# Two transformer layers in one kernel: the last part staggered by one pair, and the recurrence's running sums spread over more banks, without fillers

## The reference

```python
k_h = softmax(k_t W_in) * lr;  q_h = softmax(q_t W_in)
o_t = q_h W_out + (causal(q_h k_h^T)) v_t
W_out += k_h^T v_t
for _ in range(2):
    g_out, g_in = -attn(W_in, k_t, v_t), -attn(W_out, v_t, k_t)
    W_in, W_out = W_in - lr_in * g_in, W_out - lr_out * g_out
```

## Time and profile before

| | us |
|---|---|
| median of three runs | 2673.7 |
| the profiled execution | 2678.2 |
| its span | 2676.4 |
| TensorE busy | 2314.9 (86%) |
| VectorE busy | 1603.7 (60%) |
| ScalarE busy | 1575.9 (59%) |
| GpSimd busy | 1095.1 (41%) |
| fillers in the last part (line 966, 960 records) | 202.5 |
| fillers in the recurrence (line 814, 544 records) | 151.7 |

### The profile page before, as it was taken

One profiled execution on the slowest core, in us unless ns is written; L12 is line 12 of the kernel. 1 busy time (PEld: TensorE's weight loads), 2 busy tenths in 40 slices (PEclk: granted clock), 3 DMA queues, 4 the chain that ended last, 5 costly groups with the idle time before them and its releaser, 6 DMA issues.

```text
span 2676.4 us, 90848 instructions
## 1 busy us (share of the span) xinstructions
PE 2314.9 (86%) x33549; PEld 1456.5 (54%) x33549; DVE 1603.7 (60%) x3880; ACT 1575.9 (59%) x4079; POOL 1095.1 (41%) x1208
## 2 busy tenths in 40 slices
PE   5999994788887878886699999999999999999998
PEld 4545542455555555554367475564655656647566
DVE  2888885666666666665265474663744736537365
ACT  1878885666656666665264483563835737447365
POOL 0122221566666666667423344133332343323423
PEclk8999997888988998998899999999999999999999
DMA  5455556523322323311421302202132022220220
GB/s 173 138 156 159 156 170 143 101 51 80 78 65 67 77 64 79 74 29 33 126 48 49 88 23 78 48 26 88 30 94 47 26 70 48 76 66 26 70 48 17
DMA packets 404872, 206.35 MB, mean 77 GB/s; under 512 B 273938, under 2 KB 389778, under 8 KB 404388
## 3 DMA queue, kind: packets, MB, share of 16 engines
q1 hardware_dynamic: 404420, 200.37, 28.4%
HBM read 106.38 MB, written 71.38 MB: 66 GB/s over the span
## 4 chain that ended last, share of the span: by engine, by line
issue 33%; PE 33%; POOL 15%; DVE 9%; ACT 5%; DMA 2%; SPq 1%; POOLq 0%; DVEq 0%; ACTq 0%
POOL arena L1654 7%; PE psum L747 6%; PE psum L835 3%; DVE arena L1719 3%; PE psum L830 3%; PE psum L1013 3%; PE psum L1021 3%; ACT arena L1261 2%; PE psum L823 2%; PE psum L843 2%; PE psum L814 2%; POOL arena L1666 1%; PE psum L973 1%; PE psum L1004 1%; DVE arena L1728 1%
## 5 line engine op out<-in xcount | busy, mean ns | idle before, releaser
L1654 POOL TENSOR_TENSOR arena<-arena 128x400 f32<-128x400 f32 x256 | 218.2, 853 | 492.1 <-DVE arena L2029 492.1
L1261 ACT ACTIVATE arena<-psum,scan_sb 64x128 f32<-64x128 f32 x1152 | 308.1, 361 | 148.6 <-PE psum L904 82.7
L1445 ACT ACTIVATE arena<-psum,arena 128x100 f32<-128x100 f32 x1024 | 269.8, 366 | 6.6 <-DVE arena L2021 6.6
L1719 DVE SCALAR_TENSOR_TENSOR arena<-psum,taps_sb,arena 128x511 f32<-128x511 f32 (+2 forms) x288 | 213.7, 747 | 60.6 <-ACT arena L1170 53.8
L747 PE MATMUL psum<-arena,w_in_sb 128*128 128x512 f32 x512 | 229.9, 598 | 0.9 <-issue 0.9
L1477 POOL TENSOR_TENSOR arena<-arena 128x512 f32<-128x512 f32 x64 | 79.5, 1272 | 360.9 <-ACT arena L1196 360.9
L1501 POOL TENSOR_TENSOR arena<-arena 128x512 f32<-128x512 f32 x132 | 139.6, 1057 | 209.3 <-ACT arena L1289 209.2
L1786 DVE TENSOR_TENSOR arena<-psum,scan_sb 64x512 f32<-64x512 f32 x290 | 186.1, 674 | 36.0 <-PE psum L922 28.8
L966 PE MATMUL psum<-mask_sb,identb 128*128 128x400 bf16 x960 | 202.5, 347 | 0.0
L1437 ACT ACTIVATE arena<-psum 100x512 f32<-100x512 f32 x256 | 156.1, 610 | 49.3 <-PE psum L1087 43.0
L2021 DVE TENSOR_REDUCE arena<-psum 128x4 f32<-128x400 f32 x256 | 146.3, 573 | 62.5 <-PE psum L1074 50.8
(11 more groups left out here) (212 smaller groups left out, 4926.4 us busy)
## 6 DMA issues: line engine op xcount, KB each, us to landing
arena<-arena SPq DMA_DIRECT2D x144, 128.0 KB
arena<-x SPq DMA_DIRECT2D x32, 512.0 KB, 4.1
arena<-gates_d SPq DMA_DIRECT2D x116, 128.0 KB, 4.5
arena<-o_d SPq DMA_DIRECT2D x18, 512.0 KB, 7.3
arena<-gate_d SPq DMA_DIRECT2D x18, 512.0 KB, 8.4
v_rows_d<-arena SPq DMA_DIRECT2D x64, 136.0 KB
k_rows_d<-arena SPq DMA_DIRECT2D x64, 136.0 KB
arena<-k_rows_d SPq DMA_DIRECT2D x128, 68.0 KB, 2.0
```

The source lines that it names most:

```text
L1261: ins = act.activation(dst.rearrange("p (t x a) -> p t x a", x=PP, a=INNER)[upper, :, x], src.rearrange("p (t a) -> p t a", a=INNER)[upper ...
L1445: act.activation(c_soft[s][:, f % 2, u], sc, ACT.Exp, bias=c_max[s][:, u:u + 1]).then_inc(c_act.mark(f"exp{s}{f}u{u}"), 1)
L1654: pool.tensor_tensor(soft, soft, c_rec[s].unsqueeze(2).broadcast_to([P, 4, KEYS]), ALU.mult).then_inc(c_pool.mark(f"prob{s}{f}"), 1)
L1719: ins = dve.scalar_tensor_tensor(out=a_acc[:, t, j:TOK], in0=bank[2 + t][:, 0:TOK - j], scalar=taps_sb[:, t % KT, col:col + 1], in1=a_acc[ ...
```

## The change

In the last part the head of a pair (output projection, residual, statistics, normalisation, turn, modulation) is taken out into functions `next_...` that run for pair i + 1 inside pair i. TensorE does the projection of the next pair (`next_out`) between the down-projection and norm 2, VectorE its residual and statistics (`next_rows`) behind norm 2, and its normal form (`next_normal`) behind the mixing of layer 1; TensorE's turns (`next_turn`) stand before each slot's `vv`. The next pair has buffers of its own for its rows and statistics. SP loads the next rows after this pair's second residual, and outputs and weights during or after the attention. The first head runs before the loop, and the last pair is written out behind the loop without a successor. The turns of norm 2 go to banks 1 and 2 and stand before both value products. In a pair with a successor 58 of the 120 fillers go: those of norm 1, u1, norm 2 and vt. The fillers of the attention and of norm 3 stay. The copies that filled past sequences at the start are gone.

In the recurrence all fillers go. The sums use banks 6, 7, 5, 6, where bank 5 was the fillers'. `sums(2)` stands where sums 0 and 1 stood, `sums(3)` where 2 stood, and sums 1 and 0 of the next chunk stand in the waits at the end of a chunk; `add_state` for 2 and 3 is cut in two. GpSimd makes its products before its outputs, VectorE's mean of the outputs moves behind the maxima, and ScalarE evicts 3 before 2.

```diff
+        RUN_BANKS = (6, 7, 5, 6)
...
+            def pair(i, before, ahead, ahead2):
+
+                if before:
+                    store_rows(i - 1)
+                    load_gates_ffn(i)
+                    load_gates(i, "wv", c_wv, 3)
+                if ahead:
+                    for s in SLOTS:
+                        sp.wait_ge(c_dve.sem, c_dve.at(i, f"x2{s}1"))
+                        hold(sp)
+                        load_rows(i + 1, s)
+                    sp.wait_ge(n_pool.sem, n_pool.at(i + 1, "oz1"))
+                    hold(sp)
+                frame_values(i)
+                if ahead2:
+                    next_weights(i + 2)
+                if ahead:
...
+                            load_outputs(s, i * 2 + s + 2 * len(SLOTS))
+                    sp.wait_ge(c_pe.sem, c_pe.at(i, "wp11"))
+                    hold(sp)
+                    load_gates(i + 1, "wp", c_wp, 2)
...
-                    keep_busy(4)
...
-                    pe.wait_ge(act.sem, act.before(c, "rv3"))
-                    pe.wait_ge(pool.sem, pool.before(c, "kv0"))
-                    sums(0)
-                    pe.wait_ge(pool.sem, pool.before(c, "kv1"))
-                    sums(1)
+                    pe.wait_ge(act.sem, act.before(c, "rv2"))
+                    pe.wait_ge(pool.sem, pool.before(c, "kv2"))
+                    sums(2)
                     pe.wait_ge(act.sem, act.at(c, "e2"))
...
-                    keep_busy(1)
                     pe.wait_ge(dve.sem, dve.at(c, "wok"))
...
+
                     pe.wait_ge(act.sem, act.at(c, "rv0"))
-                    pe.wait_ge(pool.sem, pool.before(c, "kv2"))
-                    sums(2)
-                    keep_busy(1)
+                    pe.wait_ge(pool.sem, pool.before(c, "kv3"))
+                    sums(3).then_inc(mine.mark("sm3"), 1)
                     pe.wait_ge(dve.sem, dve.at(c, "xo"))
...
-                    pe.wait_ge(act.sem, act.at(c, "rv1"))
-                    pe.wait_ge(pool.sem, pool.before(c, "kv3"))
-                    sums(3)
-                    keep_busy(1)
                     pe.wait_ge(act.sem, act.at(c, "eb0"))
                     pe.transpose(bank[2][:, 3 * P:4 * P], e_b[:, 0], ident[:]).then_inc(mine.mark("tb0"), 1)
+                    add_state((2, 3), before_last, (0, 1))
                     pe.wait_ge(act.sem, act.at(c, "eb1"))
                     pe.transpose(bank[1][:, 3 * P:4 * P], e_b[:, 1], ident[:]).then_inc(mine.mark("tb1"), 1)
-                    add_state((2, 3), before_last).then_inc(mine.mark("r23"), 1)
-                    keep_busy(2)
-                    for r, b in enumerate((3, 0)):
-                        pe.wait_ge(dve.sem, dve.at(c, f"xb{r}"))
-                        pe.wait_ge(act.sem, act.at(c, f"xb{r}"))
-                        updates(grid(bank[b][:, 0:PP * ROW17], ROW17), pb_in[r], k_rows[i % 2], every).then_inc(mine.mark(f"pb{r}"), 1)
-                    keep_busy(3)
+                    pe.wait_ge(dve.sem, dve.at(c, "xb0"))
+                    pe.wait_ge(act.sem, act.at(c, "xb0"))
+                    updates(grid(bank[3][:, 0:PP * ROW17], ROW17), pb_in[0], k_rows[i % 2], every).then_inc(mine.mark("pb0"), 1)
+                    add_state((2, 3), before_last, (2, 3)).then_inc(mine.mark("r23"), 1)
+                    pe.wait_ge(dve.sem, dve.at(c, "xb1"))
+                    pe.wait_ge(act.sem, act.at(c, "xb1"))
+                    updates(grid(bank[0][:, 0:PP * ROW17], ROW17), pb_in[1], k_rows[i % 2], every).then_inc(mine.mark("pb1"), 1)
                     pe.wait_ge(dve.sem, dve.at(c, "wi1"))
                     pe.transpose(bank[2][:, 0:P], w_in_1, ident[:]).then_inc(mine.mark("ti1"), 1)
-                    keep_busy(3)
+                    pe.wait_ge(act.sem, act.at(c, "rv1"))
+                    pe.wait_ge(pool.sem, pool.at(c, "kv1"))
+                    sums(1)
                     pe.wait_ge(dve.sem, dve.at(c, "wi"))
                     pe.transpose(bank[1][:, 0:P], w_in_now, ident[:]).then_inc(mine.mark("ti"), 1)
-
-            pe.wait_ge(re_act.sem, re_act.at(CHUNKS - 1, "rv3"))
+                    pe.wait_ge(act.sem, act.at(c, "rv3"))
+                    pe.wait_ge(pool.sem, pool.at(c, "kv0"))
...
+            def next_out(n):
+
+                for s in SLOTS:
+                    pe.wait_ge(n_pool.sem, n_pool.at(n, f"wo{s}"))
+                    pe.wait_ge(n_pool.sem, n_pool.at(n, f"oz{s}"))
+                    rows_out(s, n_pe, "wo", lambda k, t: c_oz[s][:, k, tok(t)], lambda k: c_wo[s][:, k], (3, 0))
+
+            def next_turn(n, s):
+
+                pe.wait_ge(n_dve.sem, n_dve.at(n, f"xh{s}3"))
+                turn_rows(s, n_pe, "t", (2, 3))
...
+
+                for s in SLOTS:
+                    pe.wait_ge(n_act.sem, n_act.at(i, f"h{s}1"))
...
-                for s in SLOTS:
-                    pe.wait_ge(c_pool.sem, c_pool.before(i, f"wo{s}"))
-                    pe.wait_ge(c_pool.sem, c_pool.before(i, f"oz{s}"))
-                    pe.wait_ge(c_act.sem, c_act.before(i, f"kk{s}1"))
-                    rows_out(s, "wo", lambda k, t: c_oz[s][:, k, tok(t)], lambda k: c_wo[s][:, k], (2, 3))
...
-                for s in SLOTS:
-                    if s == 0:
-                        pe.wait_ge(c_dve.sem, c_dve.before(i, "rv11"))
-                        stay_warm("norm1", B(1, 1))
-                    turn_c(s, 1, (0, 1))
-                    stay_warm(f"u1{s}", B(1, 0) if s == 0 else B(0, 1))
-                    pe.wait_ge(c_act.sem, c_act.at(i, f"h1{s}1"))
-                    for k in range(KT):
-                        mm = pe.matmul(B(s, 0)[half(s)], u1_sb[:, k], c_h[s][:, k, 1:TOK + 1], start=(k == 0), stop=(k == KT - 1))
+                        mm = pe.matmul(B(s, 3)[half(s)], u1_sb[:, k], c_h[s][:, k, 1:TOK + 1], start=(k == 0), stop=(k == KT - 1))
                     mm.then_inc(c_pe.mark(f"u1{s}"), 1)
+                for s in SLOTS:
+                    pe.wait_ge(c_dve.sem, c_dve.before(i, f"rv{s}1"))
...
                                 mm.then_inc(c_pe.mark(f"v2{s}{a}"), 1)
-                for s in SLOTS:
-                    if s == 0:
-                        stay_warm("norm2", B(1, 0))
-                    turn_c(s, 2, (3, 0))
-                    stay_warm(f"vt{s}", B(1, 0) if s == 0 else B(0, 3))
+                if ahead:
+                    next_out(i + 1)
+                else:
+                    stay_warm("norm2", B(1, 0))
+                for s in SLOTS:
+                    turn_c(s, 2, (1, 2))
+                for s in SLOTS:
...
                 for s in SLOTS:
+                    if ahead:
+                        pe.wait_ge(c_act.sem, c_act.at(i, f"kk{s}1"))
+                        next_turn(i + 1, s)
                     pe.wait_ge(c_pool.sem, c_pool.at(i, f"kk{s}1"))
                     pe.wait_ge(c_act.sem, c_act.at(i, f"r{s}1"))
                     pe.wait_ge(c_pool.sem, c_pool.at(i, f"wv{s}"))
-                    rows_out(s, "vv", lambda k, t: c_kk[s][:, k, tok(t)], lambda k: c_wv[s][:, k], (0, 1))
+                    rows_out(s, c_pe, "vv", lambda k, t: c_kk[s][:, k, tok(t)], lambda k: c_wv[s][:, k], (0, 1))
+
+            with pe.Fori(0, LAST) as i:
+                pair(i, True)
...
+                        pool.wait_ge(pe.sem, pe.at(c, "sm3" if j == 3 else "r01"))
                         if j == 0:
...
+                    products(0)
+                    products(1)
                     outputs(0)
                     outputs(1)
-                    products(0)
-                    products(1)
...
+                    products(2)
+                    products(3)
                     outputs(2)
                     outputs(3)
-                    products(2)
-                    products(3)
...
-                    dve.wait_ge(pool.sem, pool.before(c, "sb3"))
-                    out_sum(o_mean, o_tok[(i - 1) % 2]).then_inc(mine.mark("osum"), 1)
-                    dve.wait_ge(mine.sem, mine.at(c, "osum"))
-                    out_mean().then_inc(mine.mark("omean"), 1)
...
+                    dve.wait_ge(pool.sem, pool.before(c, "sb3"))
+                    out_sum(o_mean, o_tok[(i - 1) % 2]).then_inc(mine.mark("osum"), 1)
...
+                        if r == 0:
+                            dve.wait_ge(mine.sem, mine.at(c, "osum"))
+                            out_mean().then_inc(mine.mark("omean"), 1)
...
+            def next_rows(n):
+
+                for s in SLOTS:
+                    dve.wait_ge(c_loaded[s], 16 * (n + 1))
...
+            def next_normal(n, s):
+
+                dve.wait_ge(n_act.sem, n_act.before(n, f"h{s}{KT - 1}"))
+                dve.tensor_copy(n_modb[s], mods(n, s)[:, 0, 0:2 * KT]).then_inc(n_dve.mark(f"modb{s}"), 1)
+                dve.wait_ge(n_dve.sem, n_dve.at(n, f"rec{s}"))
+                for t in range(TT):
+                    dve.tensor_scalar(c_xhat[s][:, t], n_x[s][:, t], n_mv[s][:, t, 0:1], n_rstd[s][:, t:t + 1],
```

(1 more changed line is left out.)

325 lines of the change are left out of this document (186 added, 139 removed).

## The result

The changed kernel takes 2537.4 us (median of four runs, 2533.1 to 2542.6) beside 2674.8 us for the kernel before on the same chip: a ratio of 0.948, 95% interval 0.945 to 0.951, 137 us less. The profiled execution took 2533.1 us with a span of 2531.3, 145.1 us under the span of before. The windows by stage of the changed kernel, columns as in rows 1: the recurrence over 31 chunks, the last part from the first up-projection, and one chunk at full clock.

What follows compares the result with a forecast made beforehand. TensorE was taken as the engine to follow in both stages, part of its busy time being fillers. 107 us (last part and ends) plus 42 us (recurrence) off the median 2673.7 us gave 2525 us; range 2450 to 2585.

Steps and rivals of the forecast that it cites:

- the last part and ends: Seven pairs with a successor, plus small estimates at start and recurrence end: together 107 us less, bounds 85 and 120.
- The head: Start of each pair in the last part: shrinks from 20.05 to 5.9 us, a gain of 14.1 us.
- The projection is hidden whole: Last part, behind the down-projection: the next pair's 7.2 us projection costs nothing, with 0.2 us left over.
- The slack of the gated outputs: Last part: GpSimd has the gated outputs ready 2.6 us before TensorE's projection asks for them.
- Rival (c): Last part: gated outputs or rows come late and everything behind the projection waits; 2577 us, chance 0.07.
- The tail of the recurrence: End of the recurrence: GpSimd finishes without two products behind it, 2 us less.
- the two small terms: Before the last part: first pair's rows loaded earlier, slots chained separately, 2 us; GpSimd without two products behind, 2 us.
- The recurrence: 32 chunks: edits in TensorE's order gain 1.3 us a chunk, 42 us; fillers' absence bounded, not added.
- the mean chunk, the clock and the issue waits: Recurrence signs: chunk 22 to 23.2 us, granted clock 0.85 to 0.92, issue waits 60 to 110 us.
- rival (a): Recurrence gives back its 1.3 us: bare waits bring more half rate, stalls stay; 2567 us, chance 0.24.
- Rival (b): Recurrence: waits take in stalls, full clock kept; chunk 19.6 to 21 us, 2429 to 2474 us, chance 0.18.
- Rival (d): Recurrence: without fillers TensorE stays at 1.2 GHz, chunk over 27.2 us; slower, 2685 us, chance 0.03.

Runs made afterwards that it cites:

- the run with ScalarE's order: Changed kernel with ScalarE's square root of slot 1 ahead of its modulation of slot 0 in the second norm: 2527.0 us, ratio 0.944.
- the two padded kernels: Changed kernel, TensorE's rounds in line, padded to 1280 instructions a chunk, 76 or 242 once ahead: 2513.2 and 2649.9 us, ratios 0.943 and 0.993.
- the first padded kernel: Changed kernel, TensorE's rounds in line, padded to 1280 instructions a chunk, 76 once ahead, first crossing at 81: 2513.2 us, ratio 0.943.
- the worse placing: Changed kernel, TensorE's rounds in line, padded to 1280 instructions a chunk, 242 once ahead, first crossing at 171: 2649.9 us, ratio 0.993.

## Why the prediction was right, and where its steps were not

Forecast were 107 us from the last part and ends, measured 110 (from the first up-projection on), plus 1.3 at the start of the recurrence, less 1.3 behind it. From the recurrence 42 were forecast, 35 measured. So 145 us of the span went where 149 were forecast; by the medians it is 137. The sum came out near in part by luck: in the last part the head won 2.2 us a pair more than forecast and the projection cost 1.8 more, and in the recurrence less than half of the gain is the new order. The pair by its steps, means over the seven pairs (v2 is the second half of the down-projection, lines 1031 and 1052; each step from start to start):

```
stretch                              before   after   forecast
up-projection to v2                   19.3    19.2
v2 to q                               19.9    21.5    -0.2
q to first scores                     15.8    15.8
first scores to kk of norm 3          79.1    78.1
kk to next up-projection              38.5    22.1    -14.1
```

**The head** was under-estimated. It lost 16.3 us, not 14.1. The two u1 products, now back to back and each on its own half of the array's columns, take 2.05 us together, where one alone took 1.93. With the waits around them 2.9 us pass from the last value product to the up-projection, where the sum had 3.7; that is 0.8 of the 1.2 us by which the new head, 4.7 us, is shorter than the 5.9 of the sum, and the turns make the rest. The other 0.9 us a pair are half-rate stretches that had stood beside the old head's wait. I had counted 3 us of them over all pairs; they were 6, and another 7 us went between the first scores and norm 3.

**The projection is hidden whole** was the step that failed in the last part: from v2 to q a pair takes 1.6 us more, 11 us in all, where I had counted 0.2 us less. The slot-1 normal form was taken over from the earlier trace rows as if it did not depend on TensorE. It does, through ScalarE: slot 1's root stands behind slot 0's modulation, which waits for the first turn, which now waits for the projection. The rows of ScalarE and VectorE, with the first turn running from 1930.96 to 1932.00, show it:

```profile
1931.60 0.78 ACT L1427 ACTIVATE arena<-psum,arena 128x512 f32<-128x512 f32 x1 [4.69 <-PE psum L990]
1932.28 0.28 ACT L1423 ACTIVATE arena<-arena,parity 128x4 f32<-128x4 f32 x1
...
1932.59 0.18 DVE L2066 RECIPROCAL arena<-arena 128x4 f32<-128x4 f32 x1 [0.95 <-ACT arena L1423]
1932.81 1.38 DVE L2069 TENSOR_SCALAR arena<-arena 128x256 f32<-128x256 f32 x4
```

So VectorE's rows of slot 1 end at 12.2 us behind the start of v2 instead of 11.4, and the wait is 2.25 us, over the 2 us that the prediction called the sign of it. The run with ScalarE's order shows the sizes: of up to 2.6 us, 0.9 are the wait, the rest is half clock, which in most pairs, not in all, falls behind this wait. At full clock the stretch takes 20.1 us, 0.4 over the forecast; the other 1.4 are half rate, for which the sum had no term here. **The slack of the gated outputs** held, with 1.6 us left instead of 2.6: GpSimd's product ends at 1922.36, the projection starts at 1923.95. Rival (c) did not happen.

```profile
1917.68 4.68 POOL L1670 TENSOR_TENSOR w_in_sb<-arena 128x1024 f32<-128x1024 f32 x2
```

**The tail of the recurrence** did not get its 2 us. From the last first turn to the first up-projection it takes 87.5 us instead of 86.2; what of the two small terms missed was not tried.

**The recurrence** gave 1.13 us a chunk for a forecast of 1.3, in the range of the mean chunk, the clock and the issue waits that were named. But the reasons were partly others. The 1.3 us were to come from the edits in the order, with the fillers' absence bounded and not added. By the four kernels with and without fillers the order alone gives 0.43 without fillers, little more than the 0.3 by which executions differ, and nothing with them; leaving the fillers out gives 0.70 in the old order and 1.21 in the new. That is the step that failed in this part: the order was counted at three times what it measures, and the stalls, which I took as they are, move. I had left them as they are because 34 fewer records were only 3% less to fetch. What counts is not the share but the remainder: a chunk of the kernel before has 1330 instructions, 50 over five pieces, so that the crossings wander over the whole chunk and eleven of 31 chunks take over 25 us; one of the changed kernel has 1297, 17 over, and within a round of eight its first crossing stays at cheap places, between about 35 and 151 behind the first turn. The same happens without any change of order in the kernel before without fillers, which has 1296. That placing can be worth this much is shown by the two padded kernels; how much of the 0.70 it is, and how much the fillers' own time, was not separated.

**Half rate** went up as the first rival said, from 3.9 to 6.1 us a chunk. Its price looks small: in a fit of a chunk's time to its half rate and its waits over 0.9 us, kernel by kernel, a microsecond of half rate goes with 0.2 to 0.36 us, 0.26 in the changed kernel. By that estimate, which no run tests by itself, 2.2 us more of it are some 0.6 us a chunk, 17 us in all: rival (a)'s mechanism is there, at less than half of the 42 us that it needed. Rival (b), stalls taken in by waits, is what the changed kernel has in part by the place of its crossings, and the first padded kernel in larger part; at 21.7 us a chunk that one is still over the 19.6 to 21 that the rival named. Rival (d) stayed far: the granted clock was 0.87. Even the worse placing gave 0.76 and 26.4 us a chunk, under its 27.2.

## What to carry to other kernels

Where issue waits show inside runs of short instructions, count the engine's instructions between them: if they stand a fixed number apart, make what is repeated a multiple of that number (here that was tried with the rounds written out in line, not in a loop) and try a few offsets before touching the work, and take no small edit's time for its own before that, since it moves them all. When a stage is moved ahead of another on one engine, follow what stands behind it in the queues of the other engines too, not only its operands. Fillers paid here where a wait stands ahead of long products, 2.0 us a pair. Between short ones the kernel was faster without them, in both orders; as leaving them out moves the crossings too, try it there and do not take it as a rule.

## What was not expected of the hardware

- Stalls of TensorE's instruction supply stand at multiples of 256 instructions where short records run without a pause, mostly 0.7 to 2.9 us long; with them moved, a chunk took 26.4 instead of 21.7 us on average. The loops add two stalls at the end of a round that stand elsewhere.
- 64 of 1297 instructions less in each chunk, a twentieth, brought nothing (22.93 against 22.77 us), while the stalls moved.
- A wait of 2.25 us ahead of full-width products had 1.6 us of half clock behind it in 34 pairs of 49 and none there in 15; one of 1.33 to 1.61 us had none there in seven pairs of seven, but five of them had it some 27 us later.
- Two groups of products with 64 weight columns each, on different halves of the columns and back to back, take 2.05 us together; one alone takes 1.93.
